# Split k of an attention block, copied to the other half of the partitions by GpSimd instead of by DMA

## What is computed

```python
def _L0_attn_ref(x, w_qkv, w_out):            # x [1, 2048, 128], w_qkv [128, 16, 192]
    qkv = jnp.einsum('bse,ehd->bshd', x, w_qkv)
    q, k, v = jnp.split(qkv, 3, axis=-1)
    logits = jnp.einsum('bqhd,bkhd->bhqk', q, k) / jnp.sqrt(64)
    logits = jnp.where(mask, logits, neg)     # mask: lower triangle
    probs = jax.nn.softmax(logits, axis=-1)
    out = jnp.einsum('bhqk,bkhd->bqhd', probs, v)
    return jnp.einsum('bshd,hde->bse', out, w_out)
```

## Time and profile before

| | |
|---|---|
| time, median of 3 runs | 1015.03 us (1014.58 to 1017.8) |
| the profiled execution | 1014.77 us |
| its span in the trace | 1012.7 us |
| TensorE busy | 947.7 us, 94% |
| VectorE busy | 710.9 us, 70% |
| ScalarE busy | 678.3 us, 67% |
| GpSimd busy | 41.2 us, 4% |
| attention | about 20 to 908 us of the span |

### The profile page before, as it was taken

How to read it: one execution, slowest core, us unless ns; L and a number is a source line. 1 busy time by engine, 2 the same in 40 slices (tenths; PEclk the granted TensorE clock), 3 DMA queues, 4 the chain that set the end, 5 groups by cost and what they waited for, 6 DMA issues and landing times.

```text
span 1012.7 us, 19075 instructions
## 1 busy us (share of the span) xinstructions
PE 947.7 (94%) x6763; PEld 739.3 (73%) x6763; DVE 710.9 (70%) x2278; ACT 678.3 (67%) x1242; POOL 41.2 (4%) x54
## 2 busy tenths in 40 slices
PE   3899999999999999999999999999999999987097
PEld 2677777777777777877777777776777777767097
DVE  4787658875887668866887478756886688735465
ACT  2877668676776757766867677676776687734075
POOL 0000000000000000000000000000000000000544
PEclk9999999999999999999999999999999999996599
DMA  9320111101210121011110121012101111021220
GB/s 212 64 53 12 27 41 40 33 7 33 64 32 12 28 63 35 10 28 42 38 33 7 34 62 32 11 33 53 42 7 33 32 33 32 7 73 37 61 60 27
DMA packets 53678, 40.03 MB, mean 40 GB/s; under 512 B 16277, under 2 KB 42689, under 8 KB 53584
## 3 DMA queue, kind: packets, MB, share of 16 engines
q1 hardware_dynamic: 52336, 36.69, 14.9%
q0 software_dynamic: 1248, 2.13, 0.7%
HBM read 18.21 MB, written 4.25 MB: 22 GB/s over the span
## 4 chain that ended last, share of the span: by engine, by line
PE 83%; DMA 5%; DVE 5%; issue 3%; POOL 2%; ACT 1%; SPq 1%; POOLq 0%; DVEq 0%
PE ps L684 26%; PE ps L712 22%; PE ps L695 21%; PE ps L663 4%; DMA k_split<-k_split 4%; PE ps L723 3%; PE ps L667 2%; PE ps L790 2%; PE ps L800 2%; POOL x_sorted L622 1%; DVE k_split L982 1%; DVE q_split L978 1%; ACT q_split L848 1%; SPq L541 1%; DMA probs<-in_L_wmod_dram 0%
## 5 line engine op out<-in xcount | busy, mean ns | idle before, releaser
L684 PE MATMUL ps<-k_split,q_split 128*128 128x512 f32 (+2 forms) x1280 | 368.4, 395 | 11.4 <-DMA k_split<-k_split 11.3
L862 ACT ACTIVATE probs<-probs,neg_max 128x128 f32<-128x128 f32 (+15 forms) x256 | 308.4, 1207 | 102.9 <-DVE neg_max L1006 102.0
L695 PE MATMUL ps<-ident,probs 128*128 128x128 f32 x2176 | 307.6, 273 | 0.2
L695 PEld LDWEIGHTS ps<-ident,probs 128*128 128x128 f32 x2176 | 258.7, 140 | 60.5 <-issue 23.0
L870 ACT COPY pT<-ps 128x512 f32<-128x512 f32 (+1 forms) x424 | 228.4, 565 | 107.9 <-PE ps L695 97.9
L999 DVE TENSOR_SCALAR_CACHE_REDUCE probs<-ps 128x512 f32<-128x512 f32 (+1 forms) x384 | 250.5, 667 | 57.5 <-PE ps L684 55.5
L712 PE MATMUL ps<-pT,v_sb 128*64 128x256 f32 (+1 forms) x2304 | 250.8, 370 | 0.0
L684 PEld LDWEIGHTS ps<-k_split,q_split 128*128 128x128 f32 x1280 | 202.9, 190 | 41.0 <-issue 15.7
L712 PEld LDWEIGHTS ps<-pT,v_sb 128*64 128x64 f32 x2304 | 157.9, 137 | 86.2 <-issue 13.3
L1002 DVE CUSTOM_DVE_ANT_0 probs<-ps,causal 128x256 f32<-128x256 f32 (+3 forms) x256 | 130.8, 511 | 21.2 <-PE ps L684 19.1
L1024 DVE COPY pT<-ps 128x512 f32<-128x512 f32 (+1 forms) x152 | 97.7, 645 | 19.5 <-PE ps L695 18.8
(11 more groups left out here) (124 smaller groups left out, 547.1 us busy)
## 6 DMA issues: line engine op xcount, KB each, us to landing
k_split<-k_split SPq DMA_DIRECT2D x64, 256.0 KB, 3.7
rinv_b<-spread_rows SPq DMA_DIRECT2D x128, 64.0 KB, 2.6
spread_rows<-rinv_rows SPq DMA_DIRECT2D x256, 0.5 KB
probs<-in_L_ffn_W_dram SPq DMA_DIRECT2D x1, 2048.0 KB, 8.7
w_pair<-in_L_attn_w_qkv_dram SPq DMA_DIRECT2D x24, 64.0 KB, 3.2
hT<-x_sorted SPq DMA_DIRECT2D x23, 65.5 KB, 2.0
x_sorted<-causal SPq DMA_DIRECT2D x1, 1495.0 KB, 13.2
x_sb<-in_L_attn_x_dram SPq DMA_DIRECT2D x4, 256.0 KB, 5.3
```

Of the source, the lines that this page charges most:

```text
L684: m = pe.matmul(ps_ring[:, s.bank, 0:w], q_split[r % 2][:, q0:q0 + P], k_split[r % 2][:, part, k0:k0 + w], start=(part == 0), stop=(part = ...
L695: m = pe.transpose(ps_turn[:, n % TURN_BANKS, P * r:P * r + P], probs[:, g % 2, r, j * P:j * P + P], ident[:])
L862: act.activation(row, row, ACT.Exp, bias=neg_max[:, g, r:r + 1], accum_out=row_sum[:, g, r:r + 1]).then_inc(exp_done, 1)
```

## The change

SP no longer issues the transfers of split k: the step "keys" goes from the sorted steps and from SP's loop, and so do SP's waits at the end. GpSimd gets a loop over all pairs and chunks ahead of its wait for the last value matmul. For each chunk it waits until VectorE has finished split k, and copies the half of head 0 and then the half of head 1, each in one instruction of 64 partitions x 2 x 512 elements. Each copy waits until the copy before it has signalled. `k_doubled[c]` now counts 1 for a copy, and TensorE's wait is changed to match. The planner's costs stay as they are, `DOUBLING` too.

```diff
--- before.py
+++ after.py
@@ -187,8 +187,6 @@
 
         steps = []
         for p in range(PAIRS):
-            for c in range(CHUNKS):
-                steps.append((self.at("lo", p, c, 1), "keys", (p, c)))
             for g in range(GROUPS):
                 steps.append((self.at("sum", p, g), "put", (p, g)))
                 steps.append((self.get_from(p, g), "get", (p, g)))
@@ -531,16 +529,7 @@
 
             for s in plan.sp:
                 p = s.key[0]
-                if s.kind == "keys":
-
-                    c = s.key[1]
-                    k_bank, k_use = plan.bank_of("proj", p, c, 1)
-                    sp.wait_ge(bank_free[k_bank], k_use + 1)
-                    cols = slice(c * BANK, (c + 1) * BANK)
-                    for h in range(2):
-                        sp.dma_start(k_split[h][own_half(1 - h), :, cols].bitcast(F32),
-                                     k_split[h][own_half(h), :, cols].bitcast(F32)).then_inc(k_doubled[c], 16)
-                elif s.kind == "put":
+                if s.kind == "put":
                     g = s.key[1]
                     n = p * GROUPS + g
                     sp.wait_ge(rinv_ready, n + 1)
@@ -572,9 +561,6 @@
                         o_bank, o_use = plan.bank_of("out", p - 2, NC - 1)
                         sp.wait_ge(bank_full[o_bank], o_use + 1)
                     load_out(p)
-            for c in range(NC):
-                sp.wait_ge(k_doubled[c], 32 * PAIRS)
-
             sp.wait_ge(rows_turned, plan.total["turn"])
             sp.dma_start(w2_rows, W2.rearrange("e d f -> d e f")).then_inc(w2_in, 16)
             sp.dma_start(experts[:, :, 2 * FF + FT:EXPERT],
@@ -609,6 +595,24 @@
                            allow_small_or_imprecise_dtypes=True).then_inc(ident_made, 1)
             nc.gpsimd.iota(spare_nos[:], pattern=[[P, SLOTS], [0, 1]], base=S, channel_multiplier=1,
                            allow_small_or_imprecise_dtypes=True).then_inc(zero_made, 1)
+            pool.wait_ge(ident_made, 8)
+            pool.wait_ge(zero_made, 1)
+            for pair in range(PAIRS):
+                for c in range(NC):
+
+                    k_bank, k_use = plan.bank_of("proj", pair, c, 1)
+                    pool.wait_ge(bank_free[k_bank], k_use + 1)
+                    cols = slice(c * BANK, (c + 1) * BANK)
+                    for h in range(2):
+                        if h:
+                            pool.wait_ge(k_doubled[c], 2 * pair + 1)
+                        elif c:
+                            pool.wait_ge(k_doubled[c - 1], 2 * pair + 2)
+                        elif pair:
+                            pool.wait_ge(k_doubled[NC - 1], 2 * pair)
+                        nc.gpsimd.tensor_copy(k_split[h][own_half(1 - h), :, cols],
+                                              k_split[h][own_half(h), :, cols]).then_inc(k_doubled[c], 1)
+            pool.wait_ge(k_doubled[NC - 1], 2 * PAIRS)
             pool.wait_ge(pv_done, plan.total["pv"])
             nc.gpsimd.memset(ones, 1.0).then_inc(sort_made, 1)
             pool.wait_ge(sort_made, 1)
@@ -672,7 +676,7 @@
                     r, c = s.key[2], s.key[3]
                     if g % 2 == 0 and r == 0 and c == 0:
 
-                        pe.wait_ge(k_doubled[g // 2], 32 * p + 32)
+                        pe.wait_ge(k_doubled[g // 2], 2 * p + 2)
                         q_bank, q_use = plan.bank_of("proj", p, g // 2, 0)
                         pe.wait_ge(bank_free[q_bank], q_use + 1)
                     if s.use:
```

## The result

The changed kernel takes 1002.3 us (median of 4 runs, 1001.96 to 1003.08) against 1014.81 us of the kernel before. The ratio is 0.987, with a 95% interval of 0.985 to 0.989: 12.5 us or 1.2% quicker. Forecast were 1008.0 us and a range of 1004 to 1018. The direction was right, the gain nearly twice what I had said, and the time lies 1.7 us under the range.

What follows compares the result with a forecast made beforehand. TensorE's order of work bounds the kernel, so only its waits for copies of split k could shrink. 5.9 us from pairs 1 to 7 plus the first chunks, together 6.9 to 7.0, gave 1008.0 us; range 1004 to 1018.

Steps and rivals of the forecast that it cites:

- allowances: Time from finished split k until TensorE would be ready for the scores: 3.96 us for most chunks 1, first chunk 1.98.
- The copy: One GpSimd copy of 64 partitions x 1024 elements: 1.65 us, from the select's row, with bounds 0.95 and 2.34.
- The hops: Signalling into GpSimd, between its two copies and out to TensorE: together about 0.35 us for a chunk.
- The worth of a stall: Pairs 1 to 7: each us of TensorE stall removed gives back 0.72 us, from a line through six periods.
- The size of the stalls: Idle time before score matmuls in pairs 1 to 7: 8.24 us, times 0.72 a gain of 5.9 us.
- The first chunk: Start of pair 0: scores 0.94 us earlier, plus 0.1 us counted for the second chunk's stall.
- The removed transfers: 64 transfers of split k and their issue on SP, 32 pairs of 1.26 us: their removal counted as nothing.
- B: Rival: GpSimd copies about as slow as the transfers, so TensorE waits similarly; 1010 to 1018 us, chance 0.17.
- C: Rival: crossing partition halves halves GpSimd's rate, about 3.2 us a copy, stalling chunks 0 and 1; 1038 us, chance 0.12.
- D: Rival: GpSimd's copies hold up VectorE between score matmuls and their PSUM banks; 1050 us, chance 0.05.
- The point from which the change loses: Latency from finished split k to scores at which stalls equal the old amount: 4.8 us, with copies of 2.2 us.
- X: Latency of one chunk's two GpSimd copies, from finished split k to first score: 3.65 us, ends 2.25 and 5.03.

Runs made afterwards that it cites:

- the run with the longer copies: Changed kernel with half of each GpSimd copy (part 0, 64 x 512) made once more ahead of the whole copy; 1003.42 us, ratio 0.9866 to the kernel before.
- the kernel that moves one part alone: Kernel before with one part of the change: GpSimd copies head 0 of a chunk, SP still transfers head 1; 1002.92 us, ratio 0.9881.
- the run with three copies: Changed kernel with every GpSimd copy made three times; 1068.36 us, ratio 1.0485 to the kernel before.

## Why the prediction was wrong, point by point

- *What bounds the kernel, where the stalls are, which allowances there are:* right. With two copies of 1.04 us every allowance of pairs 1 to 7 is met, and only the first chunk waits.
- *The copy:* 1.04 us instead of 1.65. The wrong step was to take the fill's fixed part (98 ns) off the select's row and put all that remained on the slope. A copy of 128 takes as long as the select of 128, but 181 ns of it are fixed, and the slope is the fill's (0.83 ns; I had rounded it up to 0.84). What slope the select has was not measured. The hops were 0.16, 0.06 and 0.06 us instead of 0.35 in all. The lower bound, 0.95, was nearly the truth. In the trace of the run with the longer copies this is worth 0.3 us; the times of the two kernels can't be told apart.
- *The worth of a stall:* the step that failed, together with the next one, in the term 8.24 x 0.72 = 5.9 us. I had 0.72 from a line through six periods (the fit gives 0.73); measured is 0.94 to 0.99 in each of them, against the weight loads. The line took for granted that the six pairs are alike without stalls, and the kernel after shows that they differ by 0.9 us, as much as the effect that I fitted. I should have seen it: the order of steps comes from a planner, and pair 3 also had a different pattern of stalls. This is 8.24 x 0.28 = 2.3 us. The distance of 108.5 us that I expected in every pair is 107.41 to 108.29 for the same reason.
- *The size of the stalls:* the second half of the miss, 11.1 - 8.24 = 2.8 us. The idle time in front of matmuls left out 0.24 us for each stall of these pairs, and stalls of chunks 0 of up to 0.34 us, which only the weight loads show. For pairs 1 to 7 it is 11.1 us instead of 8.24. With it, and with a worth of 1, the sum for these pairs is 11.1 instead of 5.9 us; measured are 9.64 + 0.69 us and the 0.34 at 124.79 (contained in the stretch up to chunk 1 of pair 1).
- *The first chunk:* 0.94 + 0.1 us were counted. The stretch up to chunk 1 of pair 1 is 1.94 shorter, of which 0.34 are the stall named above. With the weight loads the stalls there were 2.80 + 0.64 + 0.34 = 3.8 us, and 2.0 are left after.
- *The removed transfers:* counted at nothing, and nothing they are.
- *The range:* its low end put the stalls back whole, but from the smaller view. With the weight loads it would have been 14.5 us less what is left (1.0 and a new wait of 1.1), that is 12.4, and 1002.4.
- *The rivals:* B and C fall with the rate of the copy, D with VectorE's 667 ns. The point from which the change loses, 4.8 us, was not tried: at X = 4.46 the kernel is still 0.7% quicker than before, at 6.75 it is 4.9% slower. The price that C gave for X = 6.75, 1038, was far too low: 1068, because the stall counts whole and takes the clock with it.

## What to carry to other kernels

Read a wait of TensorE at the weight load, not at the matmul behind it, and where TensorE is busy 99% of the time, as here, count it whole. Don't fit the worth of a stall across stages that only look alike; the same stage in two kernels is the comparison that holds. From the finished split to the scores, one transfer of 256 KB between the halves took 3.2 us in one place and 4.6 in another, two took 4.5 to 6.2 us, while an idle GpSimd does the two in 2.35 us and crosses the halves for nothing. Taking away just one of the two transfers was as good.

## What the runs showed of the hardware

Behind some stalls the clock was lower as well. In the kernel before, the first weight load of the scores waited 2.80 us (at 34.24 us), and from 34 to 40 us the granted clock was 1.00. With every copy made twice it waited 3.52 us at the same place, and this is the same window (us, busy PE, PEld, DVE, ACT, POOL, then the clock):

```profile
34.00:40.00 6.00, 5.78 (x21) 5.29 (x22) 4.67 (x24) 2.76 (x10) 4.32 (x5) 0.50 0.00 0
```

0.50 is the lower of the two levels, 1.2 GHz, for all six us. In time it was not dear there: from the first split to chunk 1 of pair 1 this kernel is 3.17 us longer than the changed one, for 2.5 us more of this wait. The length of the stall alone does not decide: the kernel that moves one part alone waited only 2.2 us there, and its clock from 34 to 40 us was 0.72; the 2.42 us at 696.05 of the kernel before left it at 1.00 up to 720 us, and 2.93 us in the run with three copies were followed by 0.89. What else goes into it was not tried. For the reader of a profile it means that a wait can cost more than its length: 9.2 us for 6.1 in pair 2 with three copies. The least that a us of stall cost in the periods was 0.88, apart from the first chunk, where a longer wait took the place of another one.
